# Two-layer cross-attention on one core: one exponential for the two score products of a piece, and another opening

## The reference

```python
q = hidden_state @ Wq + bq
k = encoder_hidden_state @ Wk + bk
v = encoder_hidden_state @ Wv + bv
scores = jnp.einsum('bkgld,bksd->bkgls', q, k) * scale
scores = scores + encoder_attention_mask[:, :, None, :, :]
attn = jax.nn.softmax(scores, axis=-1)
out = jnp.einsum('bkgls,bksd->bkgld', attn, v)
out = out.transpose(0, 3, 1, 2, 4).reshape(b, l, H)
x = out @ Wo + bo + hidden_state
return (x - mu) * jax.lax.rsqrt(var + EPS) * gamma + beta
```

## Time and profile before

| | us |
|---|---|
| median of 3 runs (lowest, highest) | 1738.77 (1736.56, 1738.89) |
| the profiled execution | 1738.81 |
| its span, first to last instruction | 1737.0 |
| PE busy in the span | 1695.1 (98%) |
| DVE busy | 1267.2 (73%) |
| ACT busy | 1042.3 (60%) |
| POOL busy | 572.3 (33%) |

### The profile page before, as it was taken

One profiled execution on the slowest core, in us unless ns is written; L12 is line 12 of the kernel. 1 busy time (PEld: TensorE's weight loads), 2 busy tenths in 40 slices (PEclk: granted clock), 3 DMA queues, 4 the chain that ended last, 5 costly groups with the idle time before them and its releaser, 6 DMA issues. The chain is left out here.

```text
span 1737.0 us, 35992 instructions
## 1 busy us (share of the span) xinstructions
PE 1695.1 (98%) x10881; PEld 1005.9 (58%) x10881; DVE 1267.2 (73%) x1713; ACT 1042.3 (60%) x2370; POOL 572.3 (33%) x1169
## 2 busy tenths in 40 slices
PE   5999999999999999999999999999999999999997
PEld 3555566665565665565665565655665655656652
DVE  5567777787777777777777776777767877767776
ACT  2556666666665656665656665666656666656564
POOL 3133332333332333332333323333323333323332
PEclk8899999999999999999999999999999999999999
DMA  8546555455545465555565454455454455453541
GB/s 283 146 121 170 147 122 143 128 145 143 147 120 142 124 151 145 135 130 147 128 156 145 114 136 130 118 135 145 105 135 125 128 138 139 109 135 115 139 113 55
DMA packets 288390, 235.83 MB, mean 136 GB/s; under 512 B 140858, under 2 KB 262964, under 8 KB 288084
## 3 DMA queue, kind: packets, MB, share of 16 engines
q1 hardware_dynamic: 266852, 204.14, 43.8%
q10 hardware_dynamic: 21488, 31.06, 7.3%
HBM read 101.39 MB, written 22.02 MB: 71 GB/s over the span
## 5 line engine op out<-in xcount | busy, mean ns | idle before, releaser
L922 DVE TENSOR_REDUCE mx<-ms 128x2 f32<-128x750 f32 x896 | 809.2, 924 | 399.0 <-PE ms L1090 392.5
L740 ACT ACTIVATE probs<-sc 125x448 f32<-125x448 f32 x1522 | 744.6, 542 | 281.8 <-PE sc L1061 274.7
L1090 PE MATMUL ms<-ks,qs 96*128 96x375 bf16 (+1 forms) x2560 | 443.0, 327 | 11.4 <-DVE mx L922 8.7
L1061 PE MATMUL sc<-qs,ks 99*125 99x448 bf16 x1522 | 429.2, 358 | 6.0 <-DMA qs<-mT 3.7
L1111 PE MATMUL pv<-probs,vs 125*32 125x448 f32 x3048 | 313.2, 544 | 0.0
L1061 PEld LDWEIGHTS sc<-qs,ks 99*125 99x125 bf16 x1522 | 192.7, 137 | 204.2 <-ACT probs L740 127.8
L1090 PEld LDWEIGHTS ms<-ks,qs 96*128 96x128 bf16 (+1 forms) x2560 | 174.8, 98 | 194.3 <-issue 66.2
L1165 PE MATMUL job<-wo,on 128*112 128x512 f32 x504 | 258.2, 594 | 0.0
L936 DVE RECIPROCAL orec<-osum 128x112 f32<-128x112 f32 x256 | 213.0, 834 | 6.8 <-DMA osum<-oraw 6.8
L1183 PE MATMUL job<-xT,wq 128*128 128x224 f32 x1008 | 214.5, 356 | 0.0
L1134 PEld LDWEIGHTS job<-wv,ctxT 128*125 128x125 f32 x1536 | 191.5, 189 | 16.5 <-issue 0.3
(11 more groups left out here) (70 smaller groups left out, 1034.5 us busy)
## 6 DMA issues: line engine op xcount, KB each, us to landing
ctxT<-in_ctxT SPq DMA_DIRECT2D x64, 750.0 KB, 4.7
qs<-qp SPq DMA_DIRECT2D x756, 56.0 KB, 2.5
ks<-kp SPq DMA_DIRECT2D x765, 46.9 KB, 2.7
osum<-oraw ACTq DMA_DIRECT2D x125, 112.0 KB, 2.9
oc<-oraw ACTq DMA_DIRECT2D x125, 112.0 KB, 3.6
mask<-in_mask SPq DMA_DIRECT2D x64, 164.1 KB, 5.1
xT<-in_xT SPq DMA_DIRECT2D x32, 224.0 KB, 4.6
xin<-in_x SPq DMA_DIRECT2D x32, 224.0 KB, 3.0
```

The source lines that it names most:

```text
L740: nc.scalar.activation(probs[0:KCS, k, j, :], bank[0:KCS, 0:GL], ACT.Exp)\
L922: nc.vector.tensor_reduce(mx[o][:, cols], ms[n % 2][:, :, 0:S2], AX_X, ALU.max).then_inc(max_done[o], 1)
L1061: last = nc.tensor.matmul(bank[0:KCS, 0:GL], ks[p][0:KM, g, rows], qs[p][0:KM, g, :], start=True, stop=not masked)
L1090: last = nc.tensor.matmul(to, qs[o][0:KT, group, cols], ks[o][0:KT, group, :], start=True, stop=not masked)
```

## The change

Six things change.

1. **One exponential per piece.** `sc0` and `sc1` become one tensor of two adjacent banks, and `exp(k)` makes one ACTIVATE of 125x896 over both, in every slot but the last with scores. It waits for both products. The first product of the next piece waits for it, and the second product waits for nothing.
2. **The opening's loads.** All seven mask loads are issued by SP, right behind the first context, queries' weights and `xT`; the second context, `wv` and `bv` follow only behind 15 stack copies. ACT issues three stack copies fewer.
3. **The opening's work.** The keys of unit (1, 0) and the values of unit (0, 0) move from ahead of the flag into slot (1, -1), between its maxima, and PE waits for `wv` at that slot's start. Slot (0, 0) gets a row of its own (3): its maxima begin at piece 2 and its keys at piece 3.
4. **Matmuls whose results are not used.** `keep_clock` makes 3 products of 112x448 ahead of the first projection and 8 ahead of the flag.
5. **The weights of both layers** are issued in other portions over eight slots: at the end of (0, 0) half of `wo` and `bo` in place of seven loads of layer 1; `gamma` and `beta` of layer 0 at the end of (1, 0), four loads of layer 1 at the end of (0, 1), and the rest further on. DVE waits for `gamma` and `beta` at the start of slot (0, 1).
6. **POOL's memsets** of `ks1` and `vs1` move behind the identity matrices, so that `idd` comes earlier.

```diff
@@ tables
+CLOCK = (3, 8)
-KEYS_AT = [{2: (0,), 3: (1, 2), 4: (3,)}, {2: (0, 1), 3: (2, 3)}, {0: (0, 1, 2, 3)}]
-VALUES_AT = [{1: (0, 1), 2: (2,)}, {4: (0,), 5: (1,), 6: (2,)}, {0: (0, 1, 2)}]
+KEYS_AT = [{2: (0,), 3: (1, 2), 4: (3,)}, {2: (0, 1), 3: (2, 3)}, {0: (0,), 1: (1,), 2: (2,), 3: (3,)}]
+VALUES_AT = [{1: (0, 1), 2: (2,)}, {4: (0,), 5: (1,), 6: (2,)}, {8: (0,), 9: (1,), 10: (2,)}]
+STEPS_AT[3] = [0, 0, 2, 2, 1, 2, 1, 1, 0, 2, 0, 1]
...
@@ opening_slot (SP)
                 if p == 0:
                     stack_terms(0, 0, ks[0], kp[0], 1)
+                    stack_terms(0, 1, ks[0], kp[0], 1, of=(1, 2))
                     sp.wait_ge(q_p1[0], 2)
                     stack_terms(0, 0, qs[0], qp, 0, of=(0,))
-                    stack_terms(0, 1, ks[0], kp[0], 1, of=(1, 2))
+                    stack_terms(0, 1, ks[0], kp[0], 1, of=(0,))
+                    load_ctx(1, 0, 0)
+                    load_wv(0, w_v)
                     stack_terms(0, 1, qs[0], qp, 0, of=(0,))
...
-                    load_wo(0, w_in[0])
-                    load_rows(0, w_in[0])
+                    load_wo(0, w_in[0], slice(0, 2))
...
@@ weights (SP), was next_layer
                 if (p, i) == (0, 0):
-                    load_wk(1, w_in[1])
-                    load_wv(1, w_in[1])
-                    load_rows(1, w_in[1])
+                    load_wo(0, w_in[0], slice(2, NG))
+                    load_row(bo, 0, "bo", w_in[0])
                 if (p, i) == (1, 0):
-                    load_wq(1, w_in[1], slice(0, 2))
+                    load_row(gamma, 0, "gamma", rows_in[0])
+                    load_row(beta, 0, "beta", rows_in[0])
                 if (p, i) == (0, 1):
-                    load_wq(1, w_in[1], slice(2, DC))
+                    load_wk(1, w_in[1])
+                    load_wv(1, w_in[1])
...
@@ opening loads (SP; the two of ACT are gone)
             load_xT(1, 0, 0)
-            load_ctx(1, 0, 0)
-            load_wv(0, w_v)
-            for n in range(BEARLY, BLOADS):
+            for n in range(BLOADS):
...
@@ exp (ACT)
+                    if not last_scores(p, i):
+                        act.wait_ge(sc_ps[p], 2 * (PIECES * main + k) + 2)
+                        nc.scalar.activation(probs[0:KCS, k, :, :], sc_pair[0:KCS, :, 0:GL], ACT.Exp).then_inc(exp_done[p], 1)
+                        return
...
@@ slot (DVE)
-                if first_outputs(p, i):
-                    dve.wait_ge(w_in[0], 16 * NW[0])
+                if first_rows(p, i):
+                    dve.wait_ge(rows_in[0], 16 * NR[0])
...
@@ scores (PE)
-                            elif k > 0:
-                                pe.wait_ge(exp_done[p], 2 * (PIECES * main + k) + j - 1)
-                            elif p_ok:
-                                pe.wait_ge(exp_done[o], 2 * PIECES * (post + 1) + j - 1)
+                            elif k > 0 and j == 0 and not last_scores(p, i):
+                                pe.wait_ge(exp_done[p], exps(p, main, k))
+                            elif k == 0 and j == 0 and p_ok:
+                                pe.wait_ge(exp_done[o], PIECES * (post + 1))
...
@@ start (PE)
+            keep_clock(CLOCK[0])
             pe.wait_ge(w_k, 16 * NK)
-            for p in range(PAR):
-                slots(False, opening=True)(p, -1, exists(p, -1), layers(p, -1))
+            slots(False)(*FIRST, exists(*FIRST), layers(*FIRST))
+            keep_clock(CLOCK[1])
```

More of the change, by code:

```diff
@@ L109, in step_order @@
     return order
-ORDER = [step_order(q) for q in range(PAR + 1)]
+ORDER = [step_order(q) for q in range(len(STEPS_AT))]
 OPENS = [[min(n for at in o for n, h, _, _ in at if h == half) for half in range(2)] for o in ORDER]
@@ L173, in last_outputs, with exps @@
     return isinstance(i, int) and (p, i) == (1, UNITS)
+def exps(u, n, pieces):
+    return PIECES * n + pieces * (2 if isinstance(n, int) and (u, n) == (1, UNITS - 1) else 1)
 def need(eng, sem, value):
@@ L269, in cross_attention_two_layers @@
         yT = sb("yT", [P, D // SQ, SQ])
-        sc = [ps(f"sc{h}", [P, 512]) for h in range(2)]
+        sc_pair = ps("sc", [P, 2, 512])
+        sc = [sc_pair[:, h, :] for h in range(2)]
         ms = [ps(f"ms{h}", [P, 2, 512]) for h in range(2)]
@@ L1029, in slot @@
                     q = table_row(p, i)
[L1030 to L1032 removed]
+                    if first_values(p, i):
+                        pe.wait_ge(w_v, 16 * NV)
                     if starts_layer(p, i):
@@ L1217, in maxima @@
                         def maxima(part):
-                            for n, half, tiles, place in ORDER[q][k] if a_ok and not opening else ():
+                            for n, half, tiles, place in ORDER[q][k] if a_ok else ():
                                 if place == part:
                                     maximum(n, half, tiles, place)
-                        if k == 0 and a_ok and masked and not opening:
+                        if k == 0 and a_ok and masked:
                             pe.wait_ge(mask_in[o], 16 * (ahead + 1))
-                        if k == PIECES - 1 and a_ok and not masked and not opening:
+                        if k == PIECES - 1 and a_ok and not masked:
                             pe.wait_ge(mask_in[o], 16 * (ahead + 1))
@@ L1246, in slot @@
                             maxima(1)
-                        if k == COLUMNS_AT[q][0] and a_ok and not opening:
+                        if k == COLUMNS_AT[q][0] and a_ok:
                             max_columns(o, 0, ahead)
@@ L1254, in _, with keep_clock @@
             pe.wait_ge(idd, 3)
+            def keep_clock(times):
+                for _ in range(times):
+                    nc.tensor.matmul(ms[0][0:S, 0, 0:GL], ident4[:, 0, :], ident4[:, :, :].rearrange("p c l -> p (c l)"),
+                                     start=True, stop=True)
+            keep_clock(CLOCK[0])
             pe.wait_ge(w_k, 16 * NK)
-            for p in range(PAR):
-                slots(False, opening=True)(p, -1, exists(p, -1), layers(p, -1))
-            pe.wait_ge(idd, 3)
+            slots(False)(*FIRST, exists(*FIRST), layers(*FIRST))
+            keep_clock(CLOCK[1])
             pe.wait_ge(flag_col, BLOADS + 1)
```

118 lines of the change are left out of this document (65 added, 53 removed).

## The result

| | before | after |
|---|---|---|
| median (lowest, highest), us | 1738.83 (1736.56, 1739.17) | 1778.62 (1776.63, 1783.08) |
| runs | 4 | 4 |
| the profiled execution, us | 1738.81 | 1783.08 |
| its span, us | 1737.0 | 1781.3 |

The changed kernel is slower: the ratio is 1.0234, with a 95% interval of 1.0218 to 1.0249. That is 39.8 us, where 25.8 were forecast; the time lies in the range of 1748 to 1783. The profiled execution of after is the slowest of its four, 4.5 us above the median, and its span is 44.3 us longer than before's.

The account below looks back on a forecast made before the run. PE was taken to bound the kernel, so its added waits count one for one: 0.92 us a pair over 30.5 pairs, +28, and the opening -2.2, on 1738.81 make 1764.6 us; range 1748 to 1783.

Parts of the forecast that it names:

- the opening: Everything up to slot (1, 1), its slots and loads together: -2.2 us, from -9 to +6.
- slot (0, 1): DVE waits there for gamma and beta until 111 us and PE waits behind it: +2.1 us, bounds 0.5 and 4.
- SP's queue: Other portions of weights lengthen SP's queue ahead of an mT at four more places: +1.5 us, 0 to 3.
- The exponential: One merged ACTIVATE of 896 columns on ACT takes 0.93 us, bounds 0.76 and 0.98.
- The distance: PE needs 1.61 us from one piece to the next, 1.56 where weights load in cover; 0.92 us a pair of units.
- the first maximum: Its start in the opening, where PE waits for wv: -0.6 us, bounds -3 and +2.
- Slot (1, -1): Keys and values move in, first part at 1.2 GHz, the rest at 2.4: +2.8 us, from 0 to +6.
- slot (0, 0): Starts at full clock, but half of its maxima may wait: -1.5 us, bounds -4 and +1.
- Slot (1, 0): The 3.73 us wait for mT shrinks to about 2 and the clock drop goes: -6.5 us, bounds -8.5 and -3.
- two banks cost more together than apart: Rival: an exponential over two banks takes 1.08 us, 2.6 us a pair, 80 in all: 1815 us; chance 4%.
- the change ends faster: Rival: PE's waits at pieces 9 and 10 of p = 0 vanish: 1721 us, or 1732; chance 9%.
- the loss at the close pieces is filled by something late elsewhere: Rival: DVE catches up while PE stands, 0.3 us a pair, +9 and -7 from the opening: 1741 us; chance 6%.

Follow-up runs that it names:

- the nine and the fifteen pieces: Kernel before, one exponential only at the nine pieces with a close successor: 1783.27 us; in the other run only at the fifteen other pieces: 1747.58 us.

## Why the prediction was right, and where it was wrong

**The direction and its reason were right.** The kernel is slower because one instruction holds both banks of the scores until its end, at the places of a pair of units where the next piece wants them sooner. The runs with the nine and the fifteen pieces show this. The run with the merged exponential alone has its size: 29.2 us in (1, 1) to (1, 30) for a forecast of 28. That its whole cost, 30.0 us, is as near to 28 is luck: 5.4 us in slot (0, 31), which the forecast had at nothing, stand against 3.7 us less in slot (1, 0).

**Where the missing 14.0 us lie.** The forecast was 25.8 us, the change cost 39.8. By the table of slots, 1.4 are in the steady part (29.4 for 28), 4.6 in slot (0, 31), 8.7 in the opening (+6.5 for -2.2), and -0.7 at the end. The time is inside the range because the range was wide. The opening, with +6.5 in this execution, is just outside its own bounds of -9 to +6 (by the timed runs of the opening alone, 2.7, it is inside), and so are two of its terms, slot (0, 1) and SP's queue.

**The exponential.** 917 ns for a forecast of 0.93 us, 0.76 to 0.98 as bounds. By the Trainium skill (ScalarE: Activation LUTs, "What ACT_TABLE_LOAD costs") an ACTIVATE with immediate scale and bias takes 186 ns and 0.833 ns an element, which makes, as an estimate, 932 ns for 896 columns and 559 for 448. Measured are 917 ns after and 542 before, 15 and 17 ns less.

**The distance.** Forecast 1.61 us, with 1.56 where the weights load in cover; the held pieces of p = 0 are 1.55 to 1.61 us apart, those of p = 1 1.56 to 1.68, but for pieces 4 and 5, where ACT's casts stand between. A pair of units is 1.07 us longer in layer 0 and 1.00 in layer 1, for a forecast of 0.92. By parts: p = 0 has +0.53 (forecast 0.52), p = 1 has +0.54 and +0.47 (forecast 0.40). What was small in p = 1 is piece 5: behind piece 4's exponential and the casts of the keys it moves by 0.28 us, and 0.09 of that comes back a piece later, 0.19 for a forecast of 0.15; the held pieces 9 and 10 take 0.04 and 0.12 for 0.045 each. These are small errors of size in a sum whose parts are right.

**The last unit was left out.** "The last has its own order" was the whole treatment of the 32nd pair. Its slot (0, 31) has merged exponentials and close pieces like no other, and costs 4.6 us, of which about 2 may come with a fall of the clock that kernels without a merged exponential show there too. This step was missing, not mis-sized.

**The opening** was forecast at -2.2, and up to slot (1, 1) it is +6.5 in the profiled execution (2.7 by the timed runs of the opening alone). Term by term: the first maximum +0.3 for -0.6, released by the landing of `bv` as argued. Slot (1, -1) +4.8 for +2.8: most of the keys did run at the upper clock, but the values, from 45.38 us on, nearly all at 0.5 again; I had taken the clock to stay up once it rose. It fell at 44.45 us, ahead of the 0.7 us that PE stood for ACT's `mT` (44.69 to 45.38), so this wait didn't bring it down. Ahead of the fall PE had stood for DVE four times, 0.55 us at most, and had been busy for 5.4 us of 6.9. In the run without the idle matmuls it fell in this slot too, at 45.0 us, and the profile has no wait of PE for `mT` there. The windows of after (length, PE busy and instructions, granted clock, DMA's share, GB/s):

```profile
27.00:37.60 10.60, 3.93 (x16) 0.52 0.67 157
37.60:44.50 6.90, 5.36 (x30) 0.99 0.04 11
44.50:51.30 6.80, 6.11 (x27) 0.50 0.27 86
51.30:54.00 2.70, 1.69 (x11) 1.00 0.41 116
```

The other terms: slot (0, 0) +0.6 for -1.5: it does start at the full clock, and with the opening alone it gains 1.0, but the merged exponential takes 1.6 back. Slot (1, 0) -6.0 for -6.5, and shown by the run with the loads alone. Slot (0, 1) +6.8 for +2.1: this is the term that failed. It was outside its bounds of 0.5 to 4. DVE stood until 112.4 us where I had 111, and with PE's 2.85 us of standing came 6.8 us at half clock. The prediction had seen this same pair of things, a wait and the clock behind it, in slot (1, 0), and counted there both; in slot (0, 1) it counted the wait alone. **SP's queue with the other portions of weights**, +1.5, isn't there, and is below its bounds of 0 to 3: with the opening alone (1, 1) to (1, 30) takes 1.0 us less than before, and layer 1's pairs 52.43 us for 52.50. **The idle matmuls** did raise the clock for the first projection, by its products' lengths, and as forecast nothing of it reached the first maximum, which waits for `bv`.

**The rivals.** That two banks cost more together than apart, 1.08 us, is out with 917 ns. That the change ends faster, or that the loss at the close pieces is filled by something late elsewhere, is out with the pair of units.

## What to carry to other kernels

Merge instructions over several banks only where the next writer of those banks is further off than wait, work and hand-over together; the time the merging saves is the reader's, the time it costs is the writer's, and a saving on an engine with idle time ahead of it is worth nothing. Look for the cost in the distances between starts, since the table of waits showed 0.7 us of some 28. And put a wait for a load at its first use, not at the head of a stage: on the engine that bounds the kernel, a stand of 3.8 us cost 6.8 here, and one of 3.7 us (for `mT` in slot (1, 0)) 7.7, because the clock fell with it. It gives back only what the next wait leaves: moving the wait for `bv`, 7.4 us of standing, gave 0.8 us by the medians, which isn't told from none.

## What the hardware showed that was not expected

An ACTIVATE that raises its semaphore by two didn't take its wait along here: 756 separate semaphore instructions instead of 74, each exponential starting 96 instead of 37 ns behind its product, and 0.57 us a pair of units, 1788.5 for 1770.6 us. The Trainium skill (Trainium Kernel Development and Optimization, Key Constraints) says that compute semaphores must increment by 1. These kernels run with an increment by two as well; what the runs show is its price.

Where the granted clock fell in the opening of a trace here, PE had waited or had been idle for a part of the time ahead, and the clock could be held by work without use. With PE busy for 12.1 of the 13 us from 20 to 33 us, and for 12.8 of the next 14, it stayed at 1.00 through slot (1, -1); with 7.4 and 10.6 us it was at 0.50 there, its lower level of 1.2 GHz. The matmuls without use took none of DVE's time, which bounds that slot (it was 1.1 us shorter), and the next one was 2.5 us shorter.
